# Routed attention on one Trainium2 core: who turns the exponentials, and who weighs the values by expert

## The chip, the cores and the metric

One core of one Trainium2 chip runs the whole program. The metric is device microseconds of that core from start to end, as the median of several runs. The engines are TensorE (PE, with its weight loads as PEld), VectorE (DVE), ScalarE (ACT), GpSimd (POOL) and SyncE (SP), which issues the DMAs. Each has its own instruction stream in program order; they meet only at semaphores.

## The reference, cut to what matters

The program is a stack of eight layers on x of shape 2 x 1024 x 128. Two kinds of layer are touched. The rotary attention (`_L1_attn_a_ref`) is a softmax attention of 16 heads of 64 with 1024 keys. The routed attention (`_L1_ffn_ref`) runs twice, with 8 heads of 64 and 5 experts a head:

```python
q = einsum('bthed,bthe->bhtd', q5, sd_g); k = ...(k5, ss_g); v = ...(v5, ss_g)
attn = softmax(einsum('bhid,bhjd->bhij', q * scale, k), axis=-1)
out = einsum('bhij,bhjd->bihd', attn, v)
o5 = einsum('bthd,dm->bthm', out, Wo).reshape(b, t, H, E, DIM)
return einsum('bthem,bthe->btm', o5, md)      # md: 0 or 1, three of five experts
```

So the output of a head, divided by its softmax sum, is added into each of five expert slots whose mask is 1, over all heads, and only then multiplied by Wo.

## The kernel before

**Routed attention** (`expert_attention_stage`, names beginning with g_, run twice). A step j is one tile of 128 queries of a pair of heads; 8 steps make a unit (one pair, one batch), 8 units make 64 steps. In step j TensorE makes the scores of j+1 (L1507), up to three pairs of 320-wide fp32 projections for later units ("beside", L2303; they end when the last unit begins), and the values of step j-1 (`values`, L1549), 24 bf16 products a head. VectorE takes the maxima (L1597), multiplies the projections by gates (L2592), sums values (L2601). ScalarE takes the exponentials p (L1561). Before p can be multiplied with the values it must be turned and split into two bf16 parts. Half of each head (512 of 1024 keys) goes by DMA: ScalarE writes the high part (L1568), GpSimd subtracts it from p (L1584), SyncE issues two turning DMAs (L1593). The other half is turned by TensorE (L1522). For head 0 the split of that half is: ScalarE copies the high part (`r_hi`, L1574), TensorE subtracts it by a product with minus the identity (L1531), ScalarE copies what remains (`r_lo`, L1578). For head 1 it is an fp32 copy by ScalarE (L1574) and a subtraction by VectorE (L1603). After the values VectorE takes the reciprocals of the sums (L1609), multiplies (L1611, `o_ready`), GpSimd spreads the two heads over five experts under the mask (L2508, `route`) and adds them to z (L2512 in the first two units, L2514 and L2515 after). GpSimd also sums the gated projections (L2498 to L2500, `sum_tile`). In the last unit the finished tiles of z are turned, multiplied by Wo and added to x, one or two a step (`done_in`; L2320, L2443, L2445, L2328, L2613).

The order on an engine is written out by hand. A step of GpSimd is: subtract for both heads of step j, `sum_tile`, `route(j - 1)`. TensorE's `values(j, 0)` waits for `o_ready` of step j-1, since the sums lie in two halves of one bank.

**Rotary attention** (`attention_stage`, names beginning with at_) has 128 steps of the same kind in 16 units. Five eighths of each head go by DMA and three eighths by TensorE (L1704), and GpSimd makes both subtractions (L1755, L1762). The turned parts have three slots (`RING = 3`), but `p_hi` and `p_lo`, from which the DMAs read, have two: ScalarE's `act_hi` of step j (L1743) waits until both DMAs of step j-2 have landed. SyncE issues, for each step, the DMA of the high part, in two steps a unit the exchange of `crossed` into `swapped` (four DMAs, L1857), then the DMA of the low part. The values run two steps behind.

Of the kernel before, what the change touches and what calls it, by code (L numbers as in the profile page):

```python
# [13 lines left out]
BF16 = mybir.dt.bfloat16  # L14
# [4 lines left out]
P = 128  # L19
BATCH = 2  # L20
# [1419 lines left out]
class HeadStream:  # L1440
# [7 lines left out]

    T = SEQ // P
    GROUPS = CHUNK // P  # L1450
    BY_PE = 0

    def __init__(self, core, ctx, tag, home, sums):
# [28 lines left out]
        self.minus_ready, self.r_full, self.r_split = sem("minus_ready"), sem("r_full"), sem("r_split")  # L1482
        self.av_done = sem("av_done")
        self.recip_ready = sem("recip_ready")
        self.o_ready = sem("o_ready")
# [7 lines left out]
    def wait_split(self, eng, j, h):  # L1493

        eng.wait_ge(self.r_split if h == self.BY_PE else self.u_split, j + 1)
# [16 lines left out]
    def transpose(self, pe, j, h):  # L1512
        home = self.home(j, h)
        pe.wait_ge(self.exp_done, 2 * j + h + 1)
        before = 2 * j + h - 1
        while before >= 0 and self.home(before // 2, before % 2) != home:
            before -= 1
        if before >= 0:
            self.wait_split(pe, before // 2, before % 2)
        for k in range(self.GROUPS):  # L1520
            at = CHUNK + k * P
            ins = self.nc.tensor.matmul(self.core.ps[home][:, k * P:(k + 1) * P], self.p[:, j % 2, h, at:at + P], self.core.ident[:],  # L1522
                                        start=k == 0, stop=k == self.GROUPS - 1, is_transpose=True)
        ins.then_inc(self.u_full, 1)

    def subtract(self, pe, j):

        if j == 0:
            pe.wait_ge(self.minus_ready, 1)
        pe.wait_ge(self.u_copied, 2 * j + self.BY_PE + 1)  # L1530
        self.nc.tensor.matmul(self.core.ps[self.home(j, self.BY_PE)], self.minus[:], self.r_hi[:, j % 2], start=False, stop=True, skip_group_check=True).then_inc(self.r_full, 1)  # L1531

    def values(self, pe, j, h):
        b = j // self.T % 2
        self.wait_turned(pe, j)
        self.wait_split(pe, j, h)
        if h == 0 and j:
            pe.wait_ge(self.o_ready, j)
# [14 lines left out]
    def act_minus(self, act):  # L1553
        self.nc.scalar.activation(self.minus[:], self.core.ident[:], ACT.Copy, scale=-1.0).then_inc(self.minus_ready, 1)

    def act_exp(self, act, j, h):
        act.wait_ge(self.max_ready, 2 * j + h + 1)
        if j >= 2:
            act.wait_ge(self.lo_ready, 2 * (j - 2) + h + 1)
            act.wait_ge(self.u_full, 2 * (j - 2) + h + 1)  # L1560
# [3 lines left out]
    def act_hi(self, act, j, h):  # L1564
# [3 lines left out]
        self.nc.scalar.copy(self.p_hi[:, j % 2, h, :], self.p[:, j % 2, h, 0:CHUNK]).then_inc(self.hi_ready, 1)  # L1568

    def act_copy(self, act, j, h):  # L1570
        act.wait_ge(self.u_full, 2 * j + h + 1)
        if j >= 2:
            act.wait_ge(self.av_done, 2 * (j - 2) + h + 1)
        self.nc.scalar.copy(self.r_hi[:, j % 2] if h == self.BY_PE else self.u[:, j % 2], self.core.ps[self.home(j, h)]).then_inc(self.u_copied, 1)  # L1574

# [1779 lines left out]
```

## Time and profile before

| what | us |
|---|---|
| median of 3 runs | 2794.84 (2794.7 to 2797.34) |
| the profiled execution, its own time | 2796.8 |
| its span in the trace | 2795.0 |
| rotary attention, 694 to 1370 of the span | 676 |
| routed attention, first: steps from 1437.8; second: from 2202.6 | about 575 each |

Of the span PE is busy 87%, DVE 72%, POOL 67%, ACT 54%. "Busy" is a share of time under an instruction, and the next instruction of an engine often starts a little before the one before ends, so the length of a step is read from starts to starts. A wait in square brackets names the last instruction that released it.

### The profile page before, as it was taken

Reading aid. Unit: us, or ns where it says so; the run is one execution under the profiler, and the core shown is the slowest. Engines: PE = TensorE matmul, PEld = TensorE weight load, DVE = VectorE, ACT = ScalarE, POOL = GpSimd, SP = SyncE. Lnnn points to the kernel's source line nnn. Section 1 sums busy time; section 2 is a strip of 40 time slices with the busy share of each in tenths; the row PEclk is TensorE's granted clock in tenths of the full one; section 3 lists DMA queues with packets and bytes.
Section 4 is the critical chain, followed back from the end, with each engine's and each line's share of the span. In section 5 each row is a group of like instructions: output and inputs, shape, how many; then the busy total and the mean of one; then the engine's idle time right before and its main releaser. Section 6 shows DMA issues by size and latency. Waiting matters only on the chain. (4 is left out here: it accounts for less than half of the span.)

```text
span 2795.0 us, 57341 instructions
## 1 busy us (share of the span) xinstructions
PE 2435.0 (87%) x21637; PEld 1600.0 (57%) x21822; DVE 2010.8 (72%) x3570; ACT 1520.4 (54%) x2201; POOL 1863.8 (67%) x1738
## 2 busy tenths in 40 slices
PE   6787686796899999999788999998788889999986
PEld 3455544643566666666555666666534456666655
DVE  7998455445666767767578888887386888888873
ACT  4222122323888888888625666556453256555664
POOL 1888100001899999999647899998510578999985
PEclk9998788987999999999899999999988999999999
DMA  1000000002889898889703333333211023333333
GB/s 43 1 1 1 0 23 13 4 20 65 143 147 157 147 151 154 151 149 157 131 29 56 61 62 62 61 61 69 51 30 60 16 50 65 63 61 65 62 65 62
DMA packets 632753, 193.27 MB, mean 69 GB/s; under 512 B 614920, under 2 KB 623624, under 8 KB 632480
## 3 DMA queue, kind: packets, MB, share of 16 engines
q1 hardware_dynamic: 632480, 189.60, 36.7%
q8 instruction: 175, 2.87, 0.4%
q14 instruction: 98, 0.80, 0.1%
HBM read 20.70 MB, written 1.05 MB: 8 GB/s over the span
## 5 line engine op out<-in xcount | busy, mean ns | idle before, releaser
L2303 PE MATMUL banks<-g_w,normed_t 128*128 128x320 f32 x1536 | 502.3, 454 | 29.4 <-DVE g_scratch L2592 29.3
L1778 DVE TENSOR_REDUCE at_negmax<-banks 128x1 f32<-128x1024 f32 x256 | 301.6, 1220 | 154.4 <-PE banks L1690 154.4
L2592 DVE TENSOR_TENSOR g_scratch<-banks,g_gate 128x640 f32<-128x640 f32 x384 | 314.3, 822 | 110.5 <-PE banks L2303 108.2
L1755 POOL TENSOR_TENSOR at_p_lo<-at_p,at_p_hi 128x640 bf16<-128x640 f32 x256 | 356.7, 1405 | 25.4 <-ACT at_p_hi L1743 22.7
L1597 DVE TENSOR_REDUCE g_negmax<-banks 128x1 f32<-128x1024 f32 x256 | 310.8, 1219 | 56.5 <-PE banks L1507 56.2
L2303 PEld LDWEIGHTS banks<-g_w,normed_t 128*128 128x128 f32 x1536 | 268.2, 193 | 123.4 <-DVE g_scratch L2592 47.0
L1561 ACT ACTIVATE g_p<-banks,g_negmax 128x1024 f32<-128x1024 f32 x256 | 285.9, 1117 | 68.9 <-DVE g_negmax L1597 61.2
L1584 POOL TENSOR_TENSOR g_p_lo<-g_p,g_p_hi 128x512 bf16<-128x512 f32 x256 | 298.2, 1186 | 30.3 <-POOL g_z L2515 18.7
L1736 ACT ACTIVATE at_p<-banks,at_negmax 128x1024 f32<-128x1024 f32 x256 | 285.7, 1116 | 6.4 <-DVE at_negmax L1778 6.4
L1574 ACT CAST g_r_hi<-banks 128x512 bf16<-128x512 f32 x128 | 75.0, 586 | 378.6 <-PE banks L1522 378.6
L1690 PE MATMUL banks<-at_k_t,at_q 64*128 64x512 f32 x1024 | 258.0, 622 | 16.5 <-POOL at_k_t L2039 8.8
L1507 PE MATMUL banks<-g_k_t,g_q 64*128 64x512 f32 x1024 | 254.4, 615 | 8.0 <-ACT g_p L1561 3.0
L2508 POOL TENSOR_TENSOR g_routed<-g_o,g_mask 128x640 f32<-128x640 f32 x128 | 164.4, 1285 | 96.3 <-DVE g_o L1611 96.3
L1743 ACT CAST at_p_hi<-at_p 128x640 bf16<-128x640 f32 x256 | 186.0, 727 | 39.9 <-DMA at_t_lo<-at_p_lo 33.0
L2498 POOL TENSOR_TENSOR g_scratch<-g_scratch 128x512 f32<-128x512 f32 x122 | 159.4, 1307 | 58.7 <-DVE g_scratch L2592 58.7
L1762 POOL TENSOR_TENSOR at_u_lo<-at_u 128x768 bf16<-128x768 f32 x128 | 187.9, 1468 | 11.7 <-ACT at_u L1749 10.7
L1522 PEld LDWEIGHTS banks<-identity,g_p 128*128 128x128 f32 x1024 | 116.7, 141 | 121.8 <-issue 98.9
L1522 PE MATMUL banks<-identity,g_p 128*128 128x128 f32 x1024 | 161.8, 281 | 7.8 <-DVE g_u_lo L1603 7.3
L1568 ACT CAST g_p_hi<-g_p 128x512 bf16<-128x512 f32 x256 | 161.6, 631 | 2.8 <-DMA g_t_lo<-g_p_lo 2.7
L2601 DVE TENSOR_REDUCE g_v<-g_scratch 128x128 f32<-128x640 f32 x120 | 155.8, 1299 | 0.7
L1507 PEld LDWEIGHTS banks<-g_k_t,g_q 64*128 64x128 f32 x1024 | 88.2, 186 | 117.7 <-issue 98.1
L1549 PE MATMUL banks<-g_v_hi,g_t_hi 128*128 128x65 bf16 x1024 | 119.9, 194 | 32.5 <-DMA g_t_lo<-g_p_lo 21.3
(426 smaller groups left out, 6615.8 us busy)
## 6 DMA issues: line engine op xcount, KB each, us to landing
at_swapped<-at_crossed SPq DMA_DIRECT2D x128, 128.0 KB, 2.7
g_w<-in_ex_w SPq DMA_DIRECT2D x2, 2880.0 KB, 11.5
f_w<-in_W SPq DMA_DIRECT2D x2, 1024.0 KB, 5.7
at_rope<-in_rope SPq DMA_DIRECT2D x1, 2048.0 KB, 10.5
at_t_hi<-at_p_hi SPq DMA_TRANSPOSE x128, 3.6
at_t_lo<-at_p_lo SPq DMA_TRANSPOSE x128, 3.6
g_t_hi<-g_p_hi SPq DMA_TRANSPOSE x128, 3.1
g_t_lo<-g_p_lo SPq DMA_TRANSPOSE x128, 3.2
```

Of the source, the lines that this page charges most:

```text
L1507: ins = self.nc.tensor.matmul(self.core.ps[2 * h + half], self.q[rows, b, t * P:(t + 1) * P], self.kt[rows, b, half * CHUNK:(half + 1) * C ...
L1522: ins = self.nc.tensor.matmul(self.core.ps[home][:, k * P:(k + 1) * P], self.p[:, j % 2, h, at:at + P], self.core.ident[:], start=k == 0, ...
L1561: self.nc.scalar.activation(self.p[:, j % 2, h, :], self.core.banks[:, 2 * h:2 * h + 2, :], ACT.Exp, bias=self.negmax[:, h:h + 1]).then_in ...
L1584: self.nc.gpsimd.tensor_tensor(self.p_lo[:, j % 2, h, :], self.p[:, j % 2, h, 0:CHUNK], self.p_hi[:, j % 2, h, :], ALU.subtract).then_inc( ...
L1597: self.nc.vector.tensor_reduce(self.negmax[:, h:h + 1], self.core.banks[:, 2 * h:2 * h + 2, :], AX.XY, ALU.max, negate=True).then_inc(self ...
L1690: ins = self.nc.tensor.matmul(self.core.ps[self.pair(j, h) + half], self.q[rows, b, t * P:(t + 1) * P], self.kt[rows, b, half * CHUNK:(hal ...
L1736: self.nc.scalar.activation(self.p[:, j % 2, h, :], self.core.banks[:, first:first + 2, :], ACT.Exp, bias=self.negmax[:, j % 2, h:h + 1]). ...
L1755: self.nc.gpsimd.tensor_tensor(self.p_lo[:, j % 2, h, :], self.p[:, j % 2, h, 0:self.BY_DMA * P], self.p_hi[:, j % 2, h, :], ALU.subtract) ...
L1762: self.nc.gpsimd.tensor_tensor(self.u_lo[:, j % self.RING], self.u[:, j % self.RING], self.u_hi[:, j % self.RING], ALU.subtract).then_inc( ...
L1778: self.nc.vector.tensor_reduce(self.negmax[:, j % 2, h:h + 1], self.core.banks[:, first:first + 2, :], AX.XY, ALU.max, negate=True).then_i ...
L2303: nc.tensor.matmul(out[:, 0:ED], core.xt[:, at:at + P], w[:, kind * H + tile // (T * BATCH) * 2 + h, :], start=True, stop=True).then_inc(p ...
L2592: v.tensor_tensor(qk_product[:, tile % 2, kind] if kind < 2 else v_product[:, tile % 2], core.banks[:, bank:bank + 2, 0:ED].rearrange("p h ...
```

## The change

Routed attention. Head 0 is turned by DMA alone, all 1024 keys; head 1 keeps 512 by DMA and 512 by TensorE. The TensorE transposes, the product with minus the identity and the two ScalarE copies of head 0 go. The high part and the subtraction of head 0 are 1024 wide, and each turning DMA carries 12 blocks of 128 x 128 where it carried 8. The division and the routing are new: VectorE multiplies the mask of five experts by the reciprocal of a head, which gives `share` (`divide`), and ScalarE writes `routed` out of PSUM, one 64-wide ACTIVATE for each head and expert, ten a step (`share_out`), and raises `taken`, for which `values` now waits. GpSimd only adds to z, one step later than before (`route(j - 2)`), and the tiles of z are finished one step later (`BEHIND = 3`), so that one more is done behind the last values.

Rotary attention: `p_hi` and `p_lo` have three slots, and `act_hi`, `pool_lo` and the DMAs use slot j % 3.

```diff
-    GROUPS = CHUNK // P
-    BY_PE = 0
+    BY_PE = (0, 4)
+    BY_DMA = tuple(SEQ // P - n for n in BY_PE)
+    TURNS = (1,)
...
         if h == 0 and j:
-            pe.wait_ge(self.o_ready, j)
+            pe.wait_ge(self.taken, j)
...
-        self.nc.scalar.copy(self.p_hi[:, j % 2, h, :], self.p[:, j % 2, h, 0:CHUNK]).then_inc(self.hi_ready, 1)
+        self.nc.scalar.copy(self.p_hi[:, j % 2, self.by_dma(h)], self.p[:, j % 2, h, 0:self.BY_DMA[h] * P]).then_inc(self.hi_ready, 1)
...
-        if j >= 2:
-            self.wait_turned(act, j - 2)
-        self.nc.scalar.copy(self.p_hi[:, j % 2, h, :], self.p[:, j % 2, h, 0:self.BY_DMA * P]).then_inc(self.hi_ready, 1)
+        if j >= self.RING:
+            self.wait_turned(act, j - self.RING)
+        self.nc.scalar.copy(self.p_hi[:, j % self.RING, h, :], self.p[:, j % 2, h, 0:self.BY_DMA * P]).then_inc(self.hi_ready, 1)
...
+            def share_out(j):
+
+                act.wait_ge(share_ready, j + 1)
+                if j >= 2:
+                    act.wait_ge(z_ready, j - 1)
+                for h in range(2):
+                    at = (j % 2) * 130 + h * 65
+                    for e in range(E):
+                        ins = nc.scalar.activation(routed[:, j % 2, h, e, :], hs.sums[:, at:at + D], ACT.Copy, scale=share[:, h, e:e + 1])
+                ins.then_inc(hs.taken, 1)
...
-                pool.wait_ge(hs.o_ready, j + 1)
-                if j in (0, T, 2 * T):
-                    pool.wait_ge(mask_ready, j // T + 1)
-                step(g.tensor_tensor(routed[:], hs.o[:, unit % BATCH, t].unsqueeze(2).to_broadcast([P, 2, E, D]),
-                                     mask[:, unit // BATCH, 1, 2 * tile:2 * tile + 2, :].unsqueeze(3).to_broadcast([P, 2, E, D]), ALU.mult))
-                one, two = (routed[:, h].rearrange("p e c -> p (e c)") for h in range(2))
+                pool.wait_ge(hs.taken, j + 1)
+                one, two = (routed[:, j % 2, h].rearrange("p e c -> p (e c)") for h in range(2))
...
-                if j:
-                    route(j - 1)
-            route(STEPS - 1)
+                if j >= 2:
+                    route(j - 2)
+            for j in range(STEPS - 2, STEPS):
+                route(j)
...
+            def divide(j):
+
+                unit, t = j // T, j % T
+                tile = unit % BATCH * T + t
+                hs.dve_recip(dve, j)
+                dve.wait_ge(hs.recip_ready, j + 1)
+                if j:
+                    dve.wait_ge(hs.taken, j)
+                for h in range(2):
+                    ins = v.tensor_scalar(share[:, h, :], mask[:, unit // BATCH, 1, 2 * tile + h, :], hs.recip[:, h:h + 1], None, ALU.mult)
+                ins.then_inc(share_ready, 1)
...
-                hs.dve_lo(dve, j)
+                if j:
+                    divide(j - 1)
+                hs.dve_lo(dve, j, 1)
                 beside(2)
-                if j:
-                    hs.dve_normalise(dve, j - 1)
```

GpSimd, a step of the routed attention in its later units, before (L1584 is the subtraction for both heads, L2508 the spreading over experts):

```order
L1584 TENSOR_TENSOR g_p_lo<-g_p,g_p_hi 128x512 x2
L2498 TENSOR_TENSOR g_scratch<-g_scratch 128x4x128
L2499 TENSOR_TENSOR g_scratch<-g_scratch 128x4x64
L2500 TENSOR_TENSOR g_tok<-g_scratch 128x2x128
L2508 TENSOR_TENSOR g_routed<-g_o,g_mask 128x640
L2514 TENSOR_TENSOR g_z<-g_z,g_routed 128x320
L2515 TENSOR_TENSOR g_z<-g_z,g_routed 128x320
```

The same place now (L1580 is the subtraction):

```order
L1580 TENSOR_TENSOR g_p_lo<-g_p,g_p_hi 128x1024
L1580 TENSOR_TENSOR g_p_lo<-g_p,g_p_hi 128x512
L2505 TENSOR_TENSOR g_scratch<-g_scratch 128x4x128
L2506 TENSOR_TENSOR g_scratch<-g_scratch 128x4x64
L2507 TENSOR_TENSOR g_tok<-g_scratch 128x2x128
L2517 TENSOR_TENSOR g_z<-g_z,g_routed 128x320
L2518 TENSOR_TENSOR g_z<-g_z,g_routed 128x320
```

The 640-wide product left GpSimd, and one of its subtractions grew from 512 to 1024 columns.

ScalarE, a step of the routed attention without extra work, before:

```order
L1574 CAST g_r_hi<-banks 128x512
L1561 ACTIVATE g_p<-banks,g_negmax 128x1024
L1578 CAST g_r_lo<-banks 128x512
L1568 CAST g_p_hi<-g_p 128x512
L1561 ACTIVATE g_p<-banks,g_negmax 128x1024
L1574 COPY g_u<-banks 128x512
L1568 CAST g_p_hi<-g_p 128x512
```

and now (L1558 the exponential, L1565 the high part, L2449 the values by expert):

```order
L1558 ACTIVATE g_p<-banks,g_negmax 128x1024
L1565 CAST g_p_hi<-g_p 128x1024
L1558 ACTIVATE g_p<-banks,g_negmax 128x1024
L1574 COPY g_u<-banks 128x512
L1565 CAST g_p_hi<-g_p 128x512
L2449 ACTIVATE g_routed<-banks,g_share 128x64 x10
```

Two 512-wide copies went, one high part doubled, and ten 64-wide instructions stand at the end of the step.

TensorE between the scores and the first values of the same step, before, and then now:

```order
L1507 MATMUL banks<-g_k_t,g_q 128x512 x4
L1522 MATMUL banks<-identity,g_p 128x128 x4
L2303 MATMUL banks<-g_w,normed_t 128x320 x2
L1531 MATMUL banks<-g_r_hi,g_minus 128x512
L1549 MATMUL banks<-g_v_hi,g_t_hi 128x65
```

```order
L1512 MATMUL banks<-g_k_t,g_q 128x512 x4
L2298 MATMUL banks<-g_w,normed_t 128x320 x2
L1548 MATMUL banks<-g_v_hi,g_t_hi 128x65
L1548 MATMUL banks<-g_v_lo,g_t_hi 128x65
L1548 MATMUL banks<-g_v_hi,g_t_lo 128x65
```

The four transposes of head 0 and the product that waited for ScalarE's copy are gone from this place.

## Rows read from the trace of the kernel before

**Rows 1.** Busy time by stretch: span, PE, PEld, DVE, ACT, POOL, clock, DMA, GB/s

```profile
694.00:1370.00 676.00, 638.31 (x8657) 443.10 (x8714) 471.12 (x688) 576.03 (x685) 638.50 (x430) 0.99 0.88 149
...
1553.50:1621.65 68.15, 67.13 (x627) 44.61 (x634) 57.44 (x74) 41.17 (x61) 57.76 (x57) 1.00 0.36 63
1621.65:1690.60 68.95, 67.72 (x630) 45.12 (x638) 58.33 (x74) 41.38 (x62) 64.16 (x65) 1.00 0.32 62
2724.39:2759.97 35.58, 30.66 (x331) 21.93 (x336) 15.61 (x28) 22.17 (x44) 22.88 (x23) 1.00 0.38 73
```

**Rows 2.** Timeline of POOL, a step of routed attention: start us, us, instruction

```profile
1633.51 2.29 POOL L1584 TENSOR_TENSOR g_p_lo<-g_p,g_p_hi 128x512 bf16<-128x512 f32 x2 [0.24 <-POOL g_z L2515]
1635.76 1.27 POOL L2498 TENSOR_TENSOR g_scratch<-g_scratch 128x512 f32<-128x512 f32 x1
...
1638.60 1.26 POOL L2508 TENSOR_TENSOR g_routed<-g_o,g_mask 128x640 f32<-128x640 f32 x1
1639.93 0.86 POOL L2514 TENSOR_TENSOR g_z<-g_z,g_routed 128x320 f32<-128x320 f32 x1
...
1641.98 2.28 POOL L1584 TENSOR_TENSOR g_p_lo<-g_p,g_p_hi 128x512 bf16<-128x512 f32 x2 [0.24 <-POOL g_z L2515]
```

**Rows 3.** Timeline of PE, the same step

```profile
1636.78 1.99 PE L1507 MATMUL banks<-g_k_t,g_q 64*128 64x512 f32 x8
1638.69 0.66 PE L1522 MATMUL banks<-identity,g_p 128*128 128x128 f32 x4
1639.19 1.24 PE L2303 MATMUL banks<-g_w,normed_t 128*128 128x320 f32 x4
1640.48 0.19 PE L1549 MATMUL banks<-g_v_hi,g_t_hi 128*128 128x65 bf16 x1
...
1641.35 1.34 PE L2303 MATMUL banks<-g_w,normed_t 128*128 128x320 f32 x4
...
1644.94 0.70 PE L1507 MATMUL banks<-g_k_t,g_q 64*128 64x512 f32 x2
```

**Rows 4.** Timeline of POOL in the rotary attention, for prices by width

```profile
959.65 2.76 POOL L1755 TENSOR_TENSOR at_p_lo<-at_p,at_p_hi 128x640 bf16<-128x640 f32 x2
962.38 1.46 POOL L1762 TENSOR_TENSOR at_u_lo<-at_u 128x768 bf16<-128x768 f32 x1
...
985.26 2.35 POOL L2039 TENSOR_TENSOR at_k_t<-at_straight,at_swapped 128x1024 f32<-128x1024 f32 x1
```

**Rows 5.** Small ACT instructions: timeline; then a group, busy us and mean ns

```profile
2720.05 0.26 ACT L2445 COPY g_z_t<-banks 64x128 f32<-64x128 f32 x1
2720.20 0.58 ACT L1578 CAST g_r_lo<-banks 128x512 bf16<-128x512 f32 x1
...
L1554 ACT ACTIVATE g_minus<-identity 128x128 bf16<-128x128 f32 x2 | 0.6, 311 | 0.0
```

**Rows 6.** Waits of PE and ACT in rotary attention: total us, times, longest

```profile
PE banks L1704 <- ACT at_p L1736: 19.1, 33, 3.0
PE banks L1690 <- ACT at_p L1736: 7.6, 10, 2.4
PE banks L1889 <- ACT at_o_t L2009: 5.9, 14, 0.5
...
ACT at_p_hi L1743 <- DMA at_t_lo<-at_p_lo: 33.0, 27, 3.4
```

**Rows 7.** One such wait, timelines of SP, ACT and PE

```profile
966.98 2.51 SPq L1857 DMA_DIRECT2D at_swapped<-at_crossed  x4
...
974.35 0.73 ACT L1743 CAST at_p_hi<-at_p 128x640 bf16<-128x640 f32 x1 [2.02 <-DMA at_t_lo<-at_p_lo]
...
976.15 0.87 PE L1704 MATMUL banks<-identity,at_p 128*128 128x128 f32 x6 [1.07 <-ACT at_p L1736]
```

**Rows 8.** Last unit: exponentials, two a step, 2724.39 to 2759.97; a PE wait

```profile
L1561 ACT ACTIVATE g_p<-banks,g_negmax x8: 1116/1118/1121, 2725.6 to 2754.7; 128x1024 f32<-128x1024 f32 x8
...
2743.43 0.19 PE L1549 MATMUL banks<-g_v_hi,g_t_hi 128*128 128x65 bf16 x1 [0.50 <-ACT g_r_hi L1574]
```

More of the change, by code:

```diff
@@ L1491, in wait_turned, with turn_of, by_dma, by_pe @@
         eng.wait_ge(self.turned[j % 2], 32 * (j // 2 + 1))
-    def wait_split(self, eng, j, h):
-        eng.wait_ge(self.r_split if h == self.BY_PE else self.u_split, j + 1)
+    def turn_of(self, j, h):
+        return len(self.TURNS) * j + self.TURNS.index(h) + 1
+    def by_dma(self, h):
+        return slice(P * sum(self.BY_DMA[:h]), P * sum(self.BY_DMA[:h + 1]))
+    def by_pe(self, h):
+        return slice(P * sum(self.BY_PE[:h]), P * sum(self.BY_PE[:h + 1]))
     def fill(self, pool):
@@ L1512, in transpose @@
     def transpose(self, pe, j, h):
-        home = self.home(j, h)
+        home, n = self.home(j, h), self.turn_of(j, h)
         pe.wait_ge(self.exp_done, 2 * j + h + 1)
-        before = 2 * j + h - 1
-        while before >= 0 and self.home(before // 2, before % 2) != home:
+        before = n - 1
+        while before and self.home((before - 1) // len(self.TURNS), self.TURNS[(before - 1) % len(self.TURNS)]) != home:
             before -= 1
[L1518 to L1523, printed above, removed]
-        ins.then_inc(self.u_full, 1)
[L1526 to L1531, printed above, removed]
+        if before:
+            pe.wait_ge(self.u_split, before)
+        for k in range(self.BY_PE[h]):
+            at = (self.BY_DMA[h] + k) * P
+            ins = self.nc.tensor.transpose(self.core.ps[home][:, k * P:(k + 1) * P], self.p[:, j % 2, h, at:at + P], self.core.ident[:])
+        ins.then_inc(self.u_full, 1)
     def values(self, pe, j, h):
@@ L2184, in expert_attention_stage @@
         tok = sb("tok", [P, 2, T, 2, D])
-        routed = sb("routed", [P, 2, E, D])
+        share = sb("share", [P, 2, E])
+        routed = sb("routed", [P, 2, 2, E, D])
         z = sb("z", [P, TILES, ED])
@@ L2372, in _ @@
                     hs.scores(pe, j + 1)
-                if unit + 1 == UNITS and t > 2:
+                if unit + 1 == UNITS and t > BEHIND:
                     project_out(*done_in(t - 1)[1])
-                hs.transpose(pe, j, 0)
+                if 0 in hs.TURNS:
+                    hs.transpose(pe, j, 0)
                 for k, tile in finishing[0:1]:
@@ L2395, in _ @@
             project_out(*done_in(T - 1)[1])
-            hs.values(pe, STEPS - 1, 0)
-            turn_out(*done_in(T)[0])
-            hs.values(pe, STEPS - 1, 1)
-            project_out(*done_in(T)[0])
-            turn_out(*done_in(T + 1)[0])
-            project_out(*done_in(T + 1)[0])
+            for h in range(2):
+                hs.values(pe, STEPS - 1, h)
+            for t in range(T, T + BEHIND):
+                turn_out(*done_in(t)[0])
+                project_out(*done_in(t)[0])
         @block.scalar
@@ L2478, in _ @@
                     place_out(k)
-            for t in (T, T + 1):
+                if j:
+                    share_out(j - 1)
+            share_out(STEPS - 1)
+            for t in range(T, T + BEHIND):
                 for k, tile in done_in(t):
@@ L2675, in _ @@
                     keep(range(1, PAIRS), range(2 * T))
-            hs.dve_normalise(dve, STEPS - 1)
-            for t in (T, T + 1):
+            divide(STEPS - 1)
+            for t in range(T, T + BEHIND):
                 for k, tile in done_in(t):
```

88 lines of the change are left out of this document (41 added, 47 removed).

## The prediction

> **What bounds the kernel now.** I read busy time by stretch first [rows 1], then the timelines of the engine that is fullest in each stretch, then the waits.
>
> In the routed attention two regimes follow each other. In unit 1 (68.15 us for 8 steps) PE is under an instruction 67.13 us and POOL only 57.76. From unit 2 on, POOL adds twice to z and is at 64.16 of 68.95 us [rows 1]. There a POOL step runs start to start from 1633.51 to 1641.98, 8.47 us, and its only idle time is 0.24 us, inside its own chain of steps [rows 2]. The step of PE just beside it is 1636.78 to 1644.94, 8.16 us [rows 3]. So POOL sets units 2 to 6, with PE only 0.3 us a step behind, and PE sets units 0 and 1. An edit that relieves one of the two is worth no more than the gap to the other; this one touches both. In the last unit nobody is full: four steps [rows 8] take 35.58 us, 8.9 each, with PE at 30.66 [rows 1], held by a chain that goes back and forth between PE and ACT.
>
> In the rotary attention PE and POOL are level, 638.31 and 638.50 us of 676, and the DMA engines are at 0.88 [rows 1]. PE's idle time that ACT ends is 19.1 + 7.6 + 5.9 = 32.6 us. ACT itself waited 33.0 us for the DMA of the low part, 27 times [rows 6].
>
> **The change, routed attention, units 2 to 6 (POOL).** POOL loses L2508. Start to start that is 1638.60 to 1639.93, 1.33 us [rows 2]. It gains 512 columns in the subtraction of head 0. Two of 512 take 1633.51 to 1635.76, 1.125 each [rows 2]; two of 640 take 959.65 to 962.38, 1.365 each [rows 4]. That is 0.24 us for 128 columns, so 4 x 0.24 = 0.96 us for 512 more. The step becomes 8.47 - 1.33 + 0.96 = 8.10 us, 0.37 less. The bounds of the 1024-wide one: 2.08 us by this slope, and 2.35 by the 1024-wide fp32 sum [rows 4], with which the gain is 0.10. I take the slope, since it is the same instruction. It holds for steps 16 to 52, after which projections stop: 37 x 0.37 = 13.7 us a stage; I take 13.
>
> The GPSIMD Engine Reference of the Trainium skill (section 3.1, elementwise cycle accounting) has about 2.6 cycles an element for a two-input operation, at 1.2 GHz. By that figure 512 columns are 1.11 us rather than 0.96, and the 13 us would be 8 a stage.
>
> **Who is late next in these units.** PE loses the transposes of head 0, 1638.69 to 1639.19, 0.50 us, and the subtraction and its wait for the copy, some 0.1 us of the 1.29 us between 1639.19 and 1640.48 [rows 3]: 8.16 becomes about 7.6. Its second projection still waits until VectorE has applied the first, so no more comes off. DVE is at 58.33 us of 8 steps, 7.3 a step [rows 1]; a 128-wide product goes and two 5-wide ones come, even within 0.2. ACT is at 41.38 us, 5.2 a step [rows 1]; two 512-wide copies go (about 1.0 us), half a microsecond of high part and ten small ones come. A small one from PSUM: the 128-wide copy hands over after 0.15 us, 2720.05 to 2720.20 [rows 5]. The nearest ACTIVATE with a scale, 128 wide, lasts 0.31 [rows 5]. I take 0.16, bounds 0.10 and 0.31, so `share_out` is 1.6 us (1.0 to 3.1) and an ACT step about 6.3 (up to 7.8). All of these are under 8.10.
>
> VectorE: DVE Perf Modes of the Trainium skill (the TRN2 errata) speaks against cutting one wide operation in ten: every ScalarE instruction out of PSUM pays 172 cycles at 1.2 GHz before its elements. By it the ten are (172 + 64) / 1.2 = 197 ns each, 2.0 us; that leaves the forecast of a step and lengthens only the end.
>
> The new wait is `values` on `taken`. Its ring is: values of head 0, a projection, the transposes of head 1, values of head 1, reciprocal and `share`, `share_out`. By an estimate from the starts of this step: 0.87 + 1.2 + 0.45 + 0.75 + about 0.5 + 1.6 = 5.4 us [rows 3, 5], under 8.1 with 2.7 to spare. In it `divide` stands ahead of VectorE's subtraction for head 1; that one's reader is a step away. Behind `share_out` on ACT stands the next exponential, which needs a maximum that comes 1.2 us after the next scores, about when `share_out` ends. The DMAs carry 12 blocks instead of 8 at a share of 0.32 [rows 1]; half more is 0.48, and the values come more than a step later. I cost both at nothing, and with the cover gone they are worth 0.5 to 1 us a step.
>
> **Units 0 and 1.** The first six steps are held by VectorE, which also ranks the experts; nothing comes off. In the other ten PE sets the pace at 8.16 plus extras, and up to 0.56 us comes off each. POOL there is at 57.76 / 8 = 7.2 us [rows 1] and does not stop it. I take 0.45: 4.5 us a stage.
>
> **The last unit.** PE's 8.9 us lose 0.5 of transposes, 0.50 of waiting for the copy r_hi [rows 8], and a fraction more of waits for z_t: 7.7 in the five steps with two tiles, 1.2 each, and 0.5 in three others: 7.5 us a stage. The end: head 0's subtraction is 0.96 us longer, the DMA perhaps 0.8 (estimates from the slope above and half as many blocks more), `share_out` 1.6 stands where a 0.29 us product and the 1.33 us spreading stood, and one more tile is turned, copied, multiplied and added, 2.5 to 3 us. Against it, POOL no longer waits for VectorE's product ahead of its last subtraction, and the tile fills time in which PE waited for the DMA. I take the end as even, -2 to +3 us.
>
> Sum for a routed stage: 13 + 4.5 + 7.5 = 25 us; two stages 50.
>
> **The rotary attention.** With the third slot the 33.0 us of ACT go. In the case shown the exchange occupied SP for 2.51 us at 966.98, the low part's DMA came behind it, ACT stood 2.02 us until 974.35 and PE then 1.07 at 976.15 [rows 7]. PE gets back only what reached it. Of the 32.6 us [rows 6] I leave out about 3.5 in steps where ACT splits the values, 3.5 in the last unit, and some 4.5 (an estimate) in the first steps, where no slot is used twice yet: about 21 remain. But POOL is then the next: its 638.5 us must fit in 676 - 21 = 655, and the DMA share rises from 0.88 to 0.91. I take 16, with 8 and 22 as bounds.
>
> **Total.** 50 + 16 = 66 us. The profiled execution took 2796.8 us, so 2731; the median of the runs, 2794.84, is 2.0 lower, so 2729.
>
> **The rivals.**
> (a) The rotary slot gives nothing: POOL and DMA, both near full, take the place of the wait. For it speaks that POOL and PE have the same busy time to 0.2 us [rows 1]; against it, the idle time of both is 37 us. Then 2729 + 16 = 2745.
> (b) POOL pays the dear price, 2.35 us, for 1024 columns: the gain of units 2 to 6 is 0.10 x 37 x 2 = 7 instead of 26, giving 2748. The GPSIMD page's 2.6 cycles would be a half-way case. (a) and (b) together: 2764.
> (c) Slower than before: `share_out` becomes the bound. Each small instruction then costs t, and the ring is 3.8 + 10 t. It passes the old 8.47 when t is over 0.47 us; at 0.6 the step is 9.8, 1.3 more over about 120 steps, +156, less 16 of the rotary part: 2935. No row shows an ACT instruction this small over 0.31 us, so this is unlikely.
> (d) More than forecast: PE's steps in units 0, 1 and 7 fall by 1 us and more and the rotary part gives all 21: 2704.
> (e) Nothing in sum: the new waits take back what POOL and PE give, a step of 8.4 by a late DMA or `taken`, and a longer end. About 2790 to 2800.
>
> **How the numbers follow.** Forecast (2715 to 2740) 0.53; (a) 0.14; (b) 0.12; both 0.05; (d) 0.08; (e) 0.04; (c) 0.04. The range takes in the forecast, (a), (b), both together, and half of (d): 2706 to 2765. A measurement of this kernel tells about 0.2%, 5.6 us, from no change. Faster by more than that: everything but (c) and most of (e), 0.93; within it 0.03; slower 0.04.
>
> **What would show it.** Right: POOL's subtractions 1024 and 512 wide start 2.1 us apart; POOL's step in units 2 to 6 is 8.1; L2449 hands over in under 0.2 us; ACT's wait for the DMA in the rotary part is near zero and PE's wait for ACT under 13 us; steps of the last unit are 7.7. Wrong: values waiting for ACT (`taken`) or the DMA in the middle units, a POOL that now idles before `route`, a rotary part that still takes over 665 us.

## The result and the profile after

The changed kernel takes 2893.7 us (median of 4 runs, 2888.82 to 2896.5); the kernel before, 2796.09 (4 runs). The ratio is 1.0345, interval 1.0328 to 1.0363: 97 us slower, where 67 us faster had been forecast. A ratio, here and below, is estimated from all the runs and can differ by 0.1 per cent from the quotient of the two medians beside it. The profiled execution has a span of 2891.4 us.

The sign is decided in the routed attention. Units and steps run from the start of one exponential to the start of another (of the two a step, the first), in us, with the two stages apart where two numbers stand:

| | before | after |
|---|---|---|
| rotary attention, first to last exponential | 670.9 | 648.4 |
| routed, first exponential to last addition, per stage | 581.9, 581.9 | 642.4, 637.1 |
| of it units 2 to 6, together | 341.0, 341.1 | 381.1, 382.3 |
| most common step in units 2 to 6 | 8.17 | 9.55 |
| last unit, to the start of its last step | 57, 58 | 63, 59 |
| from there to the end of the stage | 25, 24 | 31, 30 |

The page's first part, and four of its groups (what stands last is the idle time just before them and what ended most of it):

```profile
PE 2402.1 (83%) x21182; PEld 1559.5 (54%) x21182; DVE 2188.5 (76%) x3698; ACT 1725.7 (60%) x3223; POOL 1824.8 (63%) x1610
...
L2298 PE MATMUL banks<-g_w,normed_t 128*128 128x320 f32 x1536 | 525.0, 470 | 182.6 <-DVE g_scratch L2595 182.2
...
L2449 ACT ACTIVATE g_routed<-banks,g_share 128x64 f32<-128x64 f32 x1280 | 275.6, 337 | 249.2 <-DVE g_share L2623 249.2
...
L2505 POOL TENSOR_TENSOR g_scratch<-g_scratch 128x512 f32<-128x512 f32 x122 | 158.7, 1301 | 213.3 <-DVE g_scratch L2595 213.3
...
L2623 DVE TENSOR_SCALAR g_share<-g_mask,g_recip 128x5 f32<-128x5 f32 x256 | 223.6, 917 | 4.5
```

The last row is the finding: the two small products that turn `mask` into `share`, five columns each, have a mean of 917 ns. The three rows above it are three engines that wait for VectorE: PE 182 us, ACT 249 and POOL 213. In the kernel before, projections waited 29.3 us for it. By stretch (columns as in [rows 1]), the rotary attention, and one middle unit of eight steps:

```profile
694.00:1348.00 654.00, 637.42 (x8688) 441.08 (x8687) 468.81 (x687) 578.14 (x685) 637.21 (x429) 0.99 0.91 153
...
1612.15:1688.92 76.77, 62.50 (x592) 40.20 (x591) 71.56 (x82) 53.77 (x126) 61.41 (x57) 1.00 0.44 84
```

The first answers the first of [rows 1]: the same work in 654 us, with the DMA share at the 0.91 that was forecast, and PE and POOL with as much work as before. The second answers the third: VectorE is now the fullest, 71.56 us where it had 58.33, while POOL at 61.41 and PE at 62.50 have room. One step there, timelines of DVE, POOL, ACT and PE, answering [rows 2, 3]:

```profile
1642.32 1.28 DVE L2604 TENSOR_REDUCE g_v<-g_scratch 128x128 f32<-128x640 f32 x1
1643.52 0.16 DVE L1605 RECIPROCAL g_recip<-banks 128x2 f32<-128x2 f32 x1
1643.72 2.38 DVE L2623 TENSOR_SCALAR g_share<-g_mask,g_recip 128x5 f32<-128x5 f32 x2
1646.02 0.68 DVE L1598 TENSOR_TENSOR g_u_lo<-banks,g_u 128x512 bf16<-128x512 f32 x1
1646.62 0.81 DVE L2595 TENSOR_TENSOR g_scratch<-banks,g_gate 128x640 f32<-128x640 f32 x1
...
1642.84 3.24 POOL L1580 TENSOR_TENSOR g_p_lo<-g_p,g_p_hi 128x1024 bf16<-128x1024 f32 x2 [0.24 <-POOL g_z L2518]
1647.57 1.26 POOL L2505 TENSOR_TENSOR g_scratch<-g_scratch 128x512 f32<-128x512 f32 x1 [1.49 <-DVE g_scratch L2595]
...
1652.44 3.25 POOL L1580 TENSOR_TENSOR g_p_lo<-g_p,g_p_hi 128x1024 bf16<-128x1024 f32 x2 [0.24 <-POOL g_z L2518]
...
1646.14 2.15 ACT L2449 ACTIVATE g_routed<-banks,g_share 128x64 f32<-128x64 f32 x10 [2.72 <-DVE g_share L2623]
...
1647.48 1.34 PE L2298 MATMUL banks<-g_w,normed_t 128*128 128x320 f32 x4 [1.70 <-DVE g_scratch L2595]
```

VectorE starts the pair at 1643.72 and is done at 1646.10. GpSimd's subtractions run from 1642.84 to 1646.08. Ten columns took VectorE 2.38 us, about as long as three of its 128x640 products (0.81 us each). Behind the pair come `u_lo`, then the multiplication of a projection by its gates (L2595): PE waits 1.70 us for that and GpSimd 1.49. A GpSimd step is 1642.84 to 1652.44, 9.6 us, 1.5 of it idle.

From here on an instruction "stands" when it has started and is held up, so that its time in the trace grows. Read one by one, 203 of the 256 products took over 0.25 us, and every one of the 203 ended 0.02 to 0.04 us after a GpSimd subtraction did: the first product of a pair mostly with the 1024-wide subtraction, the second with the 512-wide one. The other 53 took 0.22 us (median). Over a whole unit the pair cost 2.2 to 2.3 us a step in units 3 to 5, and 0.9 to 1.3 in units 0, 1 and 7.

### The profile page after: what moved, and what is told of

Same layout as the page of the kernel before. It is cut to its first block and busy times, and to the rows that moved or that the text cites. A ratio compares the mean times of both kernels' runs of the same rounds, so it can differ in the third digit from the quotient of the medians.

```text
span 2891.4 us, 57226 instructions
## 1 busy us (share of the span) xinstructions
PE 2402.1 (83%) x21182; PEld 1559.5 (54%) x21182; DVE 2188.5 (76%) x3698; ACT 1725.7 (60%) x3223; POOL 1824.8 (63%) x1610
## 5 line engine op out<-in xcount | busy, mean ns | idle before, releaser
L2298 PE MATMUL banks<-g_w,normed_t 128*128 128x320 f32 x1536 | 525.0, 470 | 182.6 <-DVE g_scratch L2595 182.2
L2298 PEld LDWEIGHTS banks<-g_w,normed_t 128*128 128x128 f32 x1536 | 274.1, 197 | 373.6 <-DVE g_scratch L2595 294.1
L1580 POOL TENSOR_TENSOR g_p_lo<-g_p,g_p_hi 128x1024 bf16<-128x1024 f32 (+1 forms) x256 | 426.2, 1684 | 65.6 <-ACT g_p_hi L1565 43.1
L2449 ACT ACTIVATE g_routed<-banks,g_share 128x64 f32<-128x64 f32 x1280 | 275.6, 337 | 249.2 <-DVE g_share L2623 249.2
L2595 DVE TENSOR_TENSOR g_scratch<-banks,g_gate 128x640 f32<-128x640 f32 x384 | 313.3, 819 | 91.2 <-PE banks L2298 88.1
L1558 ACT ACTIVATE g_p<-banks,g_negmax 128x1024 f32<-128x1024 f32 x256 | 285.6, 1116 | 112.5 <-DVE g_negmax L1593 107.5
L2623 DVE TENSOR_SCALAR g_share<-g_mask,g_recip 128x5 f32<-128x5 f32 x256 | 223.6, 917 | 4.5
L1565 ACT CAST g_p_hi<-g_p 128x1024 bf16<-128x1024 f32 (+1 forms) x256 | 214.8, 839 | 3.7
L1548 PE MATMUL banks<-g_v_hi,g_t_hi 128*128 128x65 bf16 x1536 | 171.4, 196 | 19.3 <-ACT g_routed L2449 14.7
L1548 PE MATMUL banks<-g_v_lo,g_t_hi 128*128 128x65 bf16 x1536 | 171.6, 196 | 0.0
L1548 PE MATMUL banks<-g_v_hi,g_t_lo 128*128 128x65 bf16 x1536 | 170.8, 196 | 0.0
L1548 PEld LDWEIGHTS banks<-g_v_hi,g_t_hi 128*128 128x128 bf16 x1536 | 145.1, 99 | 34.1 <-issue 23.7
```

What stands on the lines that cost most here:

```text
L1548: ins = self.nc.tensor.matmul(self.sums[:, at:at + 65], p, v[:, b, k, h, :], start=(k == 0 and i == 0), stop=(k == self.T - 1 and i == 2))
L1558: self.nc.scalar.activation(self.p[:, j % 2, h, :], self.core.banks[:, 2 * h:2 * h + 2, :], ACT.Exp, bias=self.negmax[:, h:h + 1]).then_in ...
L1580: self.nc.gpsimd.tensor_tensor(self.p_lo[:, j % 2, self.by_dma(h)], self.p[:, j % 2, h, 0:self.BY_DMA[h] * P], self.p_hi[:, j % 2, self.by ...
L2298: nc.tensor.matmul(out[:, 0:ED], core.xt[:, at:at + P], w[:, kind * H + tile // (T * BATCH) * 2 + h, :], start=True, stop=True).then_inc(p ...
L2449: ins = nc.scalar.activation(routed[:, j % 2, h, e, :], hs.sums[:, at:at + D], ACT.Copy, scale=share[:, h, e:e + 1])
L2595: v.tensor_tensor(qk_product[:, tile % 2, kind] if kind < 2 else v_product[:, tile % 2], core.banks[:, bank:bank + 2, 0:ED].rearrange("p h ...
```

## The experiments

**1. The same `share`, read from PSUM in one product** (label share_psum). All other parts of the change stay. `self.sums` lies in a PSUM bank.

```diff
-        self.nc.vector.reciprocal(self.recip[:], sums).then_inc(self.recip_ready, 1)
+        self.nc.vector.reciprocal(self.sums[:, 264:266], sums).then_inc(self.recip_ready, 1)
...
-                for h in range(2):
-                    ins = v.tensor_scalar(share[:, h, :], mask[:, unit // BATCH, 1, 2 * tile + h, :], hs.recip[:, h:h + 1], None, ALU.mult)
-                ins.then_inc(share_ready, 1)
+                v.tensor_tensor(share[:], mask[:, unit // BATCH, 1, 2 * tile:2 * tile + 2, :], hs.sums[:, 264:266].unsqueeze(2).to_broadcast([P, 2, E]), ALU.mult).then_inc(share_ready, 1)
```

> The changed kernel, but VectorE writes the reciprocals into free columns of the bank of the sums (PSUM), and one tensor_tensor (mask from SBUF times reciprocal from PSUM, 128x10) makes the shares in place of two tensor_scalar of 128x5. Theory (VectorE's tensor_scalar, both operands and result in SBUF, stands until the GpSimd instruction then running has ended, 2.3 us a step): an instruction with one SBUF input does not stand, it takes 0.2 us, the step of units 2 to 6 is 8.1 to 8.2 us and the whole about 2735 us. Rival (any tiny VectorE instruction that reads a value written just before costs about a microsecond here): it would take about 1 us, the step 8.5, the whole about 2790.

Measured: 2747.37 us against 2792.93 of the kernel before on that chip (19 runs), ratio 0.9829 (0.9814 to 0.9845). The tile g_share (count: lowest, median, highest ns), one middle unit, its GpSimd step:

```profile
L2622 DVE TENSOR_TENSOR g_share<-g_mask,banks x128: 165/166/168, 1455.4 to 2723.7; 128x10 f32<-128x10 f32 x128
...
1601.98:1666.79 64.81, 62.33 (x593) 40.38 (x592) 55.81 (x74) 53.33 (x125) 60.98 (x56) 1.00 0.54 96
...
1628.48 3.24 POOL L1580 TENSOR_TENSOR g_p_lo<-g_p,g_p_hi 128x1024 bf16<-128x1024 f32 x2 [0.24 <-POOL g_z L2518]
1629.48 0.17 DVE L2622 TENSOR_TENSOR g_share<-g_mask,banks 128x10 f32<-128x10 f32 x1
1636.57 3.25 POOL L1580 TENSOR_TENSOR g_p_lo<-g_p,g_p_hi 128x1024 bf16<-128x1024 f32 x2 [0.24 <-POOL g_z L2518]
```

At 1629.48 GpSimd is in the middle of the same subtraction, and the product takes 0.17 us; in all 128 steps it is within 165 to 168 ns. GpSimd's step is 8.09 us, as expected, and the whole 12 us over the 2735 expected. The change of sign, 5 per cent or some 144 us, hangs on this one edit. It does two things, one product for two and an operand in PSUM, which experiment 2 takes apart. VectorE's own time for `share` fell from 256 x 0.917 = 235 us to 128 x 0.166 = 21: 214 us went from VectorE, of which about two thirds reached the end.

**2. One product instead of two, the reciprocal still in SBUF** (share_tt). It tells the number of instructions from the place that they read.

```diff
-                for h in range(2):
-                    ins = v.tensor_scalar(share[:, h, :], mask[:, unit // BATCH, 1, 2 * tile + h, :], hs.recip[:, h:h + 1], None, ALU.mult)
-                ins.then_inc(share_ready, 1)
+                v.tensor_tensor(share[:], mask[:, unit // BATCH, 1, 2 * tile:2 * tile + 2, :], hs.recip[:].unsqueeze(2).to_broadcast([P, 2, E]), ALU.mult).then_inc(share_ready, 1)
```

> The changed kernel, but one tensor_tensor of 128x10 with both inputs in SBUF (mask times reciprocal) in place of two tensor_scalar of 128x5. Theory, if only VectorE's faster modes stand behind GpSimd: 0.2 us, step 8.1 to 8.2, whole about 2735, as with PSUM. Theory, if every VectorE instruction with two SBUF inputs stands too: one stand instead of two, 1 to 1.5 us, step about 8.6 to 8.9, whole about 2800. Rival (fixed cost of one tiny instruction): about 1 us, whole about 2790.

```profile
L2622 DVE TENSOR_TENSOR g_share<-g_mask,g_recip x128: 169/1157/1307, 1452.8 to 2768.5; 128x10 f32<-128x10 f32 x128
```

Measured: 2791.73 us, ratio 0.9993 (0.998 to 1.0005). The product of experiment 1 with its second operand in SBUF takes 1157 ns at the median, not 166. 110 of 128 took over 0.25 us, and each of them ended 0.02 to 0.03 us after a GpSimd subtraction; the other 18 took 0.17 (median). The whole alone would fit the rival with a fixed cost of about 1 us (about 2790) as well; the lengths from 0.17 to 1.31 us and their ends don't. So the place of the operand counts, and a scalar product isn't needed for it to stand. One product for two took away 102 us of the 146 by which experiment 1 is faster than the changed kernel, and the place of the operand the last 44.

**3. GpSimd's subtraction in pieces of 512** (pool_halves), with the change's own `share`. If VectorE stands until the running GpSimd instruction ends, it stands shorter behind shorter ones.

```diff
-        self.nc.gpsimd.tensor_tensor(self.p_lo[:, j % 2, self.by_dma(h)], self.p[:, j % 2, h, 0:self.BY_DMA[h] * P], self.p_hi[:, j % 2, self.by_dma(h)],
-                                     ALU.subtract).then_inc(self.lo_ready, 1)
+        first, last = self.by_dma(h).start, self.by_dma(h).stop
+        for at in range(first, last, CHUNK):
+            ins = self.nc.gpsimd.tensor_tensor(self.p_lo[:, j % 2, at:at + CHUNK], self.p[:, j % 2, h, at - first:at - first + CHUNK],
+                                               self.p_hi[:, j % 2, at:at + CHUNK], ALU.subtract)
+        ins.then_inc(self.lo_ready, 1)
```

> The changed kernel with only GpSimd's 1024-wide subtraction cut into two of 512, so that GpSimd has an end in the middle. Theory (each tensor_scalar stands until the running GpSimd instruction ends): the pair takes about 1.4 us instead of 2.3, the step falls from 9.55 to about 8.7 and the whole to 2800 to 2830 us, though GpSimd itself has one instruction more. Rival (the tensor_scalar costs 1.1 us by itself): the pair stays at 2.3 us and the whole at 2890 or a little over.

The tile, and one step, DVE and POOL:

```profile
L2626 DVE TENSOR_SCALAR g_share<-g_mask,g_recip x256: 214/736/1201, 1451.3 to 2815.1; 128x5 f32<-128x5 f32 x128
...
1655.10 1.43 DVE L2626 TENSOR_SCALAR g_share<-g_mask,g_recip 128x5 f32<-128x5 f32 x2
1654.23 3.39 POOL L1582 TENSOR_TENSOR g_p_lo<-g_p,g_p_hi 128x512 bf16<-128x512 f32 x3 [0.24 <-POOL g_z L2521]
```

Measured: 2834.91 us (2 runs), ratio 1.0145 (1.0119 to 1.0172). The mean of one went from 917 to 719 ns (the median from 1195 to 736), and 59 us went, although GpSimd has one instruction more a step (3.39 us for 3.24). The whole is a little above the 2800 to 2830 expected, and far from the rival's 2890. VectorE's instructions are the same as in the changed kernel; only GpSimd's lengths moved.

**4. Two such products in the kernel before** (before_probe). They are extra, and nothing reads them.

```diff
+        for h in range(2):
+            self.nc.vector.tensor_scalar(self.probe[:, j % 4, h, :], self.core.ident[:, 0:5], self.recip[:, h:h + 1], None, ALU.mult)
```

> The kernel before, with two tensor_scalar of 128x5 (identity times reciprocal, into a tile that nobody reads) put between VectorE's reciprocal and its product in the routed attention. Theory: each stands until the running GpSimd instruction ends; at that place GpSimd runs its 256-wide sums of 0.7 us and the 640-wide product of 1.3, so the pair takes 1 to 1.8 us, different from the 2.3 of the changed kernel, and the whole grows by 20 to 80 us. Rival (own cost of 1.1 us each): 2.3 us as in the changed kernel, the whole at 2880 to 2900.

```profile
L1613 DVE TENSOR_SCALAR g_probe<-identity,g_recip x256: 214/229/1309, 1474.2 to 2780.8; 128x5 f32<-128x5 f32 x128
```

Measured: 2801.18 us (8 runs), ratio 1.0033 (1.0021 to 1.0045), far less than the pair costs in the changed kernel, and less than the 20 to 80 us more that were expected. Only 63 of the 256 took over 0.24 us, up to 1.31, and each of these ended 0.02 to 0.03 us after a GpSimd instruction; the other 193 took 0.22. At this place mostly little of GpSimd's instruction is left, or nothing runs. The price of such an instruction is therefore not its own; it is what of GpSimd's instruction is left when it starts.

Whether the second of a pair stands too goes by what GpSimd does next. In the changed kernel the first stood in 113 of 128 steps. In 86 of these GpSimd's next subtraction followed the one before without a gap, and in all 86 the second product stood until that one ended as well; in the other 27 GpSimd's next instruction came after a gap, and the second product never stood. In experiment 3 the second stood in 89 of 89 against none of 15. In this experiment the first took over 0.25 us in 50 steps. A gap followed the GpSimd instruction in 46 of them, and the second went through in all 46; in the 4 without a gap it stood.

**5. The third slot alone** (ring_alone): the kernel before with three slots of `p_hi` and `p_lo` in the rotary attention. The same change of the wait stands for GpSimd, and slots are taken as j % RING.

```diff
-        self.p_hi, self.p_lo = (sb(n, [P, 2, 2, self.BY_DMA * P], BF16) for n in ("p_hi", "p_lo"))
+        self.p_hi, self.p_lo = (sb(n, [P, self.RING, 2, self.BY_DMA * P], BF16) for n in ("p_hi", "p_lo"))
...
-        if j >= 2:
-            self.wait_turned(act, j - 2)
+        if j >= self.RING:
+            self.wait_turned(act, j - self.RING)
```

> The kernel before with only the third slot of p_hi and p_lo in the rotary attention. Theory (the two parts of the change are independent, and the traces show 22.5 us less between the first and the last exponential of the rotary stage): units of 40.8 us instead of about 42, the whole about 22 us under the kernel before, 2770 to 2775, ratio 0.992. Rival (the earlier end only moves a wait into the next stage): under 8 us.

Measured: 2771.58 us against 2795.64 (9 runs) on that chip, ratio 0.9912 (0.989 to 0.9933). Its rotary attention lasts 648.4 us, its routed stages are as before (580.7 and 581.5). From the third to the last but one every unit is 40.8 us, where they were 40.9 to 43.5. The first is 41.3 for 46.3, but it was 42.1 in the trace of experiment 4, whose rotary attention is also that of the kernel before and lasts 666.2 us. So the traces put the gain at 18 to 23 us.

**6. Experiment 1 without the third slot** (psum_ring2).

> The kernel with the reciprocals in PSUM, with the two slots of before in the rotary attention: the routed part of the change alone, without its wait. Theory: the rotary stage is back at about 670 us, the whole at 2747 + 22 = 2769, 25 us under before (3 us a unit in ten units, little elsewhere).

Measured: 2769.38 us, ratio 0.9906 (0.988 to 0.9931); rotary 670.9 us as before. The two halves add up within their intervals: 0.88 and 0.94 per cent apart, 1.71 together.

**7. The last unit** (tail_first). In experiment 1 the late steps of the last unit are still 8.9 us (one 10.5), with 7.7 forecast. The place, timelines of DVE, PE and ACT in share_psum, rows of one step and the start of the next:

```profile
2692.98 0.29 DVE L2626 TENSOR_TENSOR residual<-residual,banks 128x128 f32<-128x128 f32 x1 [1.65 <-PE banks L2323]
...
2697.67 0.29 DVE L2626 TENSOR_TENSOR residual<-residual,banks 128x128 f32<-128x128 f32 x1 [2.00 <-PE banks L2323]
2697.88 1.22 DVE L1593 TENSOR_REDUCE g_negmax<-banks 128x1 f32<-128x1024 f32 x1
...
2691.82 1.13 PE L2323 MATMUL banks<-g_wo,g_z_t 128*128 128x128 f32 x6 [0.89 <-ACT g_z_t L2439]
...
2690.24 1.11 ACT L1558 ACTIVATE g_p<-banks,g_negmax 128x1024 f32<-128x1024 f32 x1 [1.86 <-DVE g_negmax L1593]
2691.25 0.36 ACT L2437 COPY g_z_t<-banks 128x256 f32<-128x256 f32 x1
```

The addition to `residual` waits for PE's product (L2323); the maximum comes behind the addition; the exponential waits 1.86 us for the maximum; the copies of z_t (L2437, L2439) come behind the exponential; and PE's next product waits 0.89 us for the copies. That is a ring, and none of what the change removes lies in it. The edit puts the first finished tile's copies ahead of the exponential, on ACT's queue alone:

```diff
+                for k, tile in finishing[0:1]:
+                    place_out(k)
                 if not last:
                     hs.act_exp(act, j + 1, 0)
-                for k, tile in finishing[0:1]:
-                    place_out(k)
```

> The kernel with the reciprocals in PSUM, and in the last unit of the routed attention ScalarE's two copies of the turned tile of z (place_out of the first tile) ahead of the next exponential instead of behind it. Theory: the steps of 8.9 us in the last unit are a ring: product with Wo, VectorE's add, the maximum behind it, exponential, the two copies, product, add, turning, values, scores, product. With the copies ahead of the exponential, maximum and exponential leave the ring and the steps become 7.9 to 8.4 us, the whole 4 to 9 us less than with the reciprocals in PSUM alone (about 2739). Rival (the forecast's reading, TensorE's own work and its wait for copies of head 0 made the 8.9): the steps stay at 8.9 and the whole the same within 2 us.

```profile
2681.15 0.37 ACT L2437 COPY g_z_t<-banks 128x256 f32<-128x256 f32 x1 [1.17 <-PE banks L2315]
2681.62 1.11 ACT L1558 ACTIVATE g_p<-banks,g_negmax 128x1024 f32<-128x1024 f32 x1
...
2688.95 0.37 ACT L2437 COPY g_z_t<-banks 128x256 f32<-128x256 f32 x1 [0.70 <-PE banks L2315]
2689.41 1.12 ACT L1558 ACTIVATE g_p<-banks,g_negmax 128x1024 f32<-128x1024 f32 x1
```

Measured: 2738.25 us (5 runs), ratio 0.9796 (0.9774 to 0.9819). The exponential no longer waits, and steps of this kind are 7.8 us (here 2681.62 to 2689.41). This is the fastest version of the study, 2 per cent under the kernel before; its interval overlaps that of experiment 1 slightly, and in the traces its stages are 7.4 and 2.4 us shorter than there, 3.5 and 5.1 us shorter than in experiment 6 with the same routed code. One execution differs from the next by single steps of about 1.6 us (10.47 for 8.89 in the last unit).

**8. Which small instructions stand** (forms). Experiment 1 with four extra instructions beside `share`, which nothing reads.

```diff
+                v.tensor_scalar(form_b[:, j % 4, 0:2], hs.sums[:, 264:266], 2.0, None, ALU.mult)
                 v.tensor_tensor(share[:], mask[:, unit // BATCH, 1, 2 * tile:2 * tile + 2, :], hs.sums[:, 264:266].unsqueeze(2).to_broadcast([P, 2, E]), ALU.mult).then_inc(share_ready, 1)
+                own = mask[:, unit // BATCH, 1, 2 * tile, :]
+                v.tensor_reduce(form_a[:, j % 4, 0:1], own, AX.X, ALU.add)
+                v.tensor_copy(form_c[:, j % 4, 0:5], own)
+                v.tensor_scalar(form_d[:, j % 4, 0:5], own, 2.0, None, ALU.mult)
```

> The kernel with the reciprocals in PSUM, with four more tiny VectorE instructions in each step, whose results nobody reads: b, a tensor_scalar from PSUM to SBUF ahead of the shares; then a, a tensor_reduce, c, a tensor_copy and d, a tensor_scalar with a constant, all three from SBUF to SBUF, 5 elements wide. GpSimd's subtraction runs at that time. Theory (instructions that can run in a faster mode of VectorE, with operand and result in SBUF, stand until GpSimd's instruction ends; the pointer operand is not the reason): a and b take about 0.15 to 0.2 us, c and d stand, at least the first of them up to 2 us. Rival (only the pointer operand to a fresh value makes it stand): all four take under 0.25 us.

```profile
L2626 DVE TENSOR_REDUCE g_form_a<-g_mask x128: 150/151/153, 1456.2 to 2778.6; 128x1 f32<-128x5 f32 x128
L2623 DVE TENSOR_SCALAR g_form_b<-banks x128: 159/160/162, 1456.0 to 2778.5; 128x2 f32<-128x2 f32 x128
L2627 DVE COPY g_form_c<-g_mask x128: 160/1009/1091, 1456.3 to 2778.7; 128x5 f32<-128x5 f32 x128
L2628 DVE TENSOR_SCALAR g_form_d<-g_mask x128: 154/157/1165, 1457.0 to 2778.7; 128x5 f32<-128x5 f32 x128
```

A single run, 2802.82 us. The reduction out of SBUF and the product out of PSUM never stand. The copy SBUF to SBUF stands like `share` did: 101 of 128 were held up, and each of these ended 0.02 to 0.03 us after a GpSimd subtraction. It doesn't read the reciprocal, so a pointer operand to a fresh value isn't needed. The product with a constant, right behind the copy, stood 9 times. In 77 steps the copy had stood until the end of one subtraction and the next followed without a gap, and the follower went through all the same, where in the changed kernel it stood in 86 of 86. Why it goes through here and not there stays open.

## Why the prediction was wrong, step by step

**VectorE (the step that failed).** The prediction wrote that "a 128-wide product goes and two 5-wide ones come, even within 0.2". They cost 2.2 to 2.3 us a step together in units 3 to 5 (2.38 in the step shown), where even the two alone are 0.43: they stand until GpSimd's running instruction is over, and the change sets them under GpSimd's longest one. With 7.3 us of VectorE a step forecast to fit under 8.10, another 2.2 pass it, and the period goes to 9.55. Experiments 1 to 4 show it from four sides: another place of the operand, half as many, shorter GpSimd instructions, the same instructions at another place.

Rival (c) had the right sign, from another mechanism: it made ACT's ten small instructions the bound. They took 2.15 us, inside the bounds of 1.0 to 3.1, and ACT waited 249 us for `share`; values waited for ACT only in the last unit, not in the middle ones. That the sign of (c) came true is luck. The price of VectorE's ten columns was taken from their width alone. A row of the kernel before, not read then, had the sign, DVE and POOL side by side:

```profile
1609.02 1.99 DVE L1621 TENSOR_TENSOR g_v_lo<-g_v,g_v_hi 128x1040 bf16<-128x1040 f32 x1
...
1608.64 1.28 POOL L2498 TENSOR_TENSOR g_scratch<-g_scratch 128x512 f32<-128x512 f32 x1
1609.99 1.60 POOL L2499 TENSOR_TENSOR g_scratch<-g_scratch 128x256 f32<-128x256 f32 x1
1611.68 0.73 POOL L2500 TENSOR_TENSOR g_tok<-g_scratch 128x256 f32<-128x256 f32 x1
```

L2500, 128x256 on POOL, takes 0.73 us; L2499, as wide, took 1.60, while VectorE's `v_lo`, with two inputs in SBUF, ran to 1611.01. And `v_lo`, started 1609.02, had POOL's L2498 before it until 1609.92. Read after experiments 1 to 4, these rows say that the two engines hold each other up in both directions. They are no single case: 15 of the sums L2498 to L2500 in this trace took over 1.3 times the shortest of their line, and all 15 ran beside a VectorE product of two SBUF inputs.

The Trainium skill has the rule: SBUF — State Buffer, "Who interferes with whom", says that VectorE and GpSimd share a port pair as an exclusive lock for a whole instruction. VectorE's copies and scalar products can want it, and so does an instruction with both inputs in SBUF beside a GpSimd instruction that reads SBUF; a reduction doesn't, nor any instruction with at most one SBUF input outside the two-port modes. The traces agree for all of these: medians of 1195, 1009 and 1157 ns (scalar product, copy, two SBUF inputs) against 151, 160 and 166 (reduction, scalar product out of PSUM, one input in PSUM). The follower of experiment 8, 157 ns, is the one that the rule doesn't tell. It was the rule that spoke against this change, and the prediction weighed two others.

**GpSimd, units 2 to 6.** "The step becomes 8.10 us": in experiment 1, where VectorE doesn't stand, it is 8.09, and 1024 and 512 columns together take 3.24 us, as by the slope (2.08 + 1.12). Rival (b) with 2.35 falls. Units 2 to 6 gave 341.0 - 327.5 = 13.5 and 341.1 - 325.9 = 15.2 us there, for 13 forecast. But the two regimes were nearly one: by the exponentials the most common step was 8.17 in unit 1 and in unit 3 alike, and is 7.78 in both. GpSimd's own step in units 2 to 6 fell from 8.47 to 8.09. Which of the two engines gave the 13.5 and 15.2 us isn't shown.

The Trainium skill's 2.6 cycles an element (GPSIMD Engine Reference, section 3.1) would make 512 more columns 1.11 us and the step 8.25, as an estimate. The trace, with 8.09, bears out the slope of 0.96.

**PE late next, about 7.6.** A little low: PE is busy 62.33 us in a unit of experiment 1, 7.8 a step. Of the 8.17 a step, 0.39 came off, for 0.56 forecast.

**ACT.** `share_out`: 2.15 us for ten, starts 0.196 apart (median), each 0.337 long; 0.16 had been taken. It changed nothing in the middle.

By VectorE: DVE Perf Modes of the Trainium skill (the TRN2 errata) the estimate was 197 ns each. The measured 196 ns from start to start agree.

**Units 0 and 1: mis-sized.** Forecast 4.5 us a stage; experiment 1 gave 0.2 and 1.4. In unit 1 common steps fell from 8.17 to 7.78, but the third step grew from 7.63 to 9.29, and in unit 0, of steps "held by VectorE", the second grew from 10.12 to 10.61. The third there was 9.58 and is 10.65 in one stage and 9.48 in the other, which is most of what tells the stages apart. In the step before the one that grew in unit 1, `v_lo` took 2.31 us for 1.99 before; but it took 2.32 in unit 2 too, where the third step is 8.03. The cause stays open.

**Last unit and end: the mechanism was wrong.** Forecast 7.5 us a stage from 8.9 to 7.7 a step. The transposes and the wait for `r_hi` did go, but PE waited longer for the ring of experiment 7: it stood idle 12.4 us in the last unit, for 9.1 and 9.9 before. In experiment 1 the last unit to the start of its last step is 0.6 and 2.9 us shorter than before, and the end behind it 2.4 and 3.5 us longer, for -2 to +3 forecast: together 1.8 and 0.6 us longer. The "0.50 of waiting for the copy" in [rows 8] was a wait at one place of a ring that another edge set. With that edge cut, the steps are 7.8.

**Rotary attention: the mechanism right, the size low, 22.5 us for 16.** That is at the upper bound of 22, and (a) falls: POOL and DMA, at 637 of 654 us and 0.91, didn't take the place of the wait. ACT's wait for the DMA of the low part [rows 6] is gone. The waits that take its place, in the changed kernel, same stretch:

```profile
PE banks L1683 <- ACT at_p L1729: 8.3, 11, 2.4
PE banks L1697 <- ACT at_p L1729: 5.0, 16, 1.3
ACT at_u L1742 <- PE banks L1697: 51.6, 98, 2.8
ACT at_o_t L2002 <- PE banks L1922: 11.4, 28, 0.6
```

PE's waits for ACT are 13.3 us for 32.6 before, where "under 13 us" was asked for. ACT's for PE (the last two rows) are no idle time of PE; they were 46.7 and 9.8 us before. PE's idle time as a whole fell from 676 - 638.3 = 37.7 to 654 - 637.4 = 16.6 us.

**The sum.** Forecast 66 us, as 16 + 2 x (13 + 4.5 + 7.5). With `share` at its forecast price (experiment 1) the kernel gives 0.0171 x 2795 = 48 us: 22.5 for the rotary part and 12 and 16 for the stages by the traces, 50.6. So apart from `share` the forecast gain was 15 to 18 us too large. That 2747 lies in the range of 2706 to 2765 owes something to errors that offset each other: 6.5 us too little for the rotary part against 7.5 a stage for the last unit that did not come. With `share` as it was, 2893.7 lies far outside.

## What to carry to other kernels

Before a small VectorE instruction is added, look at what GpSimd runs at that place: SBUF-to-SBUF copies and scalar products, and products of two SBUF tensors, can cost what is left of GpSimd's instruction, however narrow they are, and two in a row can cost two such instructions where GpSimd's follow without a gap. Let one operand come from PSUM (the reciprocal was computed from a PSUM row anyway), set them where GpSimd rests, or keep GpSimd's instructions short. And where no engine is full, find the ring before counting what leaves it: a shorter step in it is worth nothing if it doesn't lie on the edge that is late.

## What the runs showed of the hardware

- A 128x5 VectorE product from SBUF to SBUF took 0.22 us alone and up to 1.31 us under a GpSimd instruction, and ended 0.03 us after that. In the other direction a GpSimd sum of 0.73 us took 1.60.
- The second of two such products stood as well in 86 of 86 cases where GpSimd's next instruction followed without a gap, and in none of 27 where a gap came first.
- VectorE instructions with one operand in PSUM never stood: 128x10 in 165 to 168 ns, 128 times out of 128, at the place where 110 of 128 stood with the operand in SBUF. Nor did a reduction out of SBUF (150 to 153 ns).
- ACT with a scale per partition, 64 columns out of PSUM: 0.196 us from start to start, 0.337 long.
- GpSimd, f32 less bf16 into bf16: 1024 and 512 columns in 3.24 us, three of 512 in 3.39: cutting one in two cost 0.15 us.
